# Causal attentions of a one-core transformer: the mask under the row maxima added by VectorE in the scores' bank instead of by TensorE's mask products

## The reference

```python
B_, S, D = (2, 256, 256); H = 16; HD = D // H
q = (x @ Wq.T).reshape(b, s, H, HD)
k = (x @ Wk.T).reshape(b, s, H, HD)
v = (x @ Wv.T).reshape(b, s, H, HD)
scores = jnp.einsum('bqhd,bkhd->bhqk', q, k) / np.sqrt(HD).astype(np.float32)
causal = jnp.tril(jnp.ones((s, s), bool))
scores = jnp.where(causal, scores, jnp.finfo(scores.dtype).min)
probs = jax.nn.softmax(scores, axis=-1)
out = jnp.einsum('bhqk,bkhd->bqhd', probs, v).reshape(b, s, d)
return out @ Wo.T
```

## Time and profile before

| what | value |
|---|---|
| runs of the kernel before | 2774.63, 2782.56, 2786.53 us, median 2782.56 |
| profiled execution | 2789.25 us, its span 2787.5 us |
| busy over the span: TensorE, VectorE, ScalarE, GpSimd | 2531.3, 1627.8, 1259.5, 1289.6 us |
| mean granted clock of TensorE | 0.928 of 2.4 GHz |
| layer 0's causal attention, first reduction to last maxima | about 57 to 226 us |
| layer 1's causal attention, the same | about 1458.5 to 1629 us |

### The profile page before, as it was taken

The page is one execution under the profiler, slowest core; times in us unless marked ns, Lnnn a source line. Parts: engine busy times, 40 slices in busy tenths (PEclk is TensorE's granted clock), DMA queues, the critical chain, the costliest instruction groups (busy, mean ns, idle before and its releaser), DMA issues. The chain is left out here.

```text
span 2787.5 us, 40697 instructions
## 1 busy us (share of the span) xinstructions
PE 2531.3 (91%) x14471; PEld 1686.6 (61%) x14474; DVE 1627.8 (58%) x2168; ACT 1259.5 (45%) x2174; POOL 1289.6 (46%) x1130
## 2 busy tenths in 40 slices
PE   6887999878999999999878888789999989998798
PEld 4444777654444444444664446578888867776676
DVE  4663555577666766664436633477767745554555
ACT  4464333464555555555334552256555543333222
POOL 4100344486888888888521003254545523442243
PEclk9798999898999999999976979899999998998799
DMA  1000111121101101010000001100100001110111
GB/s 58 1 2 15 35 46 48 44 79 38 39 16 38 39 24 38 16 35 1 27 24 1 1 1 49 52 22 20 31 20 20 21 10 41 45 45 15 30 42 41
DMA packets 39709, 81.63 MB, mean 29 GB/s; under 512 B 7552, under 2 KB 21120, under 8 KB 39040
## 3 DMA queue, kind: packets, MB, share of 16 engines
q1 hardware_dynamic: 39264, 79.41, 10.2%
q10 hardware_dynamic: 288, 0.13, 0.0%
HBM read 59.07 MB, written 2.62 MB: 22 GB/s over the span
## 5 line engine op out<-in xcount | busy, mean ns | idle before, releaser
L2017 DVE TENSOR_REDUCE a1h_mseg<-bank 128x2 f32<-128x1024 f32 x256 | 302.7, 1222 | 187.3 <-PE bank L1774 173.4
L63 POOL TENSOR_TENSOR f_wh<-f_raw,ones_r 128x768 fp32r<-128x768 f32 (+1 forms) x74 | 111.8, 1511 | 545.6 <-PE bank L464 367.2
L1951 ACT ACTIVATE a1h_prob<-bank 128x512 f32<-128x512 f32 x366 | 206.1, 598 | 165.8 <-PE bank L1834 83.8
L1754 POOL TENSOR_TENSOR a_qk<-a_qk,a1h_prob 128x512 f32<-128x512 f32 x186 | 238.7, 1315 | 50.8 <-ACT a1h_prob L1951 50.8
L453 PE MATMUL bank<-x_norm_h,f_wh 128*128 128x512 f32 x592 | 244.2, 412 | 6.5 <-PEq L3247 2.5
L453 PE MATMUL bank<-x_norm_l,f_wh 128*128 128x512 f32 x592 | 238.7, 403 | 0.0
L453 PE MATMUL bank<-x_norm_h,f_wl 128*128 128x512 f32 x592 | 237.5, 401 | 0.0
L656 DVE SCALAR_TENSOR_TENSOR f_tf<-bank,f_bias,f_sg 128x512 f32<-128x512 f32 x148 | 111.0, 751 | 191.8 <-PE bank L453 185.4
L1832 PE MATMUL bank<-a1h_ql,a1h_k 128*128 128x512 f32 x512 | 203.2, 397 | 0.0
L544 ACT ACTIVATE f_hhi<-f_hf 128x512 fp32r<-128x512 f32 x124 | 78.3, 632 | 276.3 <-DVE f_hf L664 276.3
L1847 PE MATMUL bank<-a1h_prob,a_v 128*64 128x512 f32 x732 | 179.8, 604 | 0.0
(11 more groups left out here) (595 smaller groups left out, 6337.8 us busy)
## 6 DMA issues: line engine op xcount, KB each, us to landing
f_raw<-in_l_w_dram SPq DMA_DIRECT2D x66, 385.0 KB, 3.1
a1h_st_q<-a_qk SPq DMA_DIRECT2D x128, 128.0 KB, 2.4
l2a_qkraw<-in_l2a_wqk_dram SPq DMA_DIRECT2D x32, 128.0 KB, 2.1
l2a_vraw<-in_l2a_wvg_dram SPq DMA_DIRECT2D x8, 512.0 KB, 3.8
f_raw<-in_l_w_dram SPq DMA_DIRECT2D x8, 449.0 KB, 3.3
a_qk<-l_keys SPq DMA_DIRECT2D x24, 128.0 KB, 2.8
a1p_raw<-in_l1a_w_dram SPq DMA_DIRECT2D x20, 128.0 KB, 2.1
a_qk<-in_l1a_wo_dram SPq DMA_DIRECT2D x16, 128.0 KB, 2.1
```

Of the source, the lines that this page charges most:

```text
L63: return pool.tensor_tensor(dst, src, one.to_broadcast(list(src.shape)), ALU.mult)
L1754: pool.tensor_tensor(out, first, slot_of[t % NP], ALU.add).then_inc(sum_done, 1)
L1951: act.activation(slot_of[t % NP], core.bank[2 + t % 3][:, :], ACT.Exp, scale=scale).then_inc(p_ready, 1)
L2017: dve.tensor_reduce(mseg[:, :, qb, s], spare(("A", n, k))[:, :, :], AX.X, ALU.max).then_inc(a_read, 1)
```

## The change

In a diagonal visit TensorE issues no mask products for the maxima any more. Each pair is announced by its score products. VectorE first adds a constant tile `later` (128 x 128, 0 on and under the diagonal, -1e30 above it, the same for both heads) to the last 128 columns of both heads, in their bank, waits for that addition, and then reduces as before. `later` is made by GpSimd with a memset and an affine select among the other constants.

```diff
@@ attend_causal
+        later_added, cleared = sem("later_added"), sem("cleared")
+        later = sb("later", [P, P])
@@ masks(pool, written)
             pool.memset(mpos[:, :, :, :].bitcast(F32), 0.0).then_inc(made, 1)
+            pool.memset(later[:, :], 0.0).then_inc(cleared, 1)
+            pool.wait_ge(cleared, 1)
+            pool.affine_select(later[:, :], later[:, :], [[-1, P]], ALU.is_ge, -1e30, base=0,
+                               channel_multiplier=1).then_inc(made, 1)
@@
+        def diagonals(x):
+            return sum(seg(y)[3] for y in range(x))
@@ maxima(x) on TensorE
-                                       kt[rows, 2 * (Q % SLOTS) + p, s * HALF:s * HALF + n], start=True, stop=not diag,
+                                       kt[rows, 2 * (Q % SLOTS) + p, s * HALF:s * HALF + n], start=True, stop=True,
                                        tile_position=(64 * u, 0))
-                    if not diag:
-                        mm.then_inc(a_ready, 1)
-                    elif x < 4:
-                        mask_pair(x, p, n)
-                if diag and x >= 4:
-                    for p in range(2):
-                        mask_pair(x, p, n)
-
-            def mask_pair(x, p, n):
-
-                ps = spare(("A", x, p))
-                for c in range(2):
-                    for u in range(2):
-                        mm = mask(pe, ps[:, u, n - P + 64 * c:n - P + 64 * c + 64], 0, c, u)
-                mm.then_inc(a_ready, 1)
+                    mm.then_inc(a_ready, 1)
@@ maxima(x) on VectorE
                     dve.wait_ge(a_ready, use["A", x, p] + 1)
+                    if diag:
+                        part = spare(("A", x, p))[:, :, n - P:n]
+                        dve.tensor_tensor(part, part, later[:, :].unsqueeze(1).to_broadcast([P, 2, P]),
+                                          ALU.add).then_inc(later_added, 1)
+                        dve.wait_ge(later_added, 2 * diagonals(x) + p + 1)
```

## The result

The changed kernel takes 2811.1 us, median of 6 runs (2802.9 to 2820.9), beside 2786.0 us of the kernel before on the same chip. The medians are 25.1 us apart, 0.90%. The changed kernel is slower, clear of noise. Forecast was 2789.5 us, no change that can be told, with a range up to 2807. The profiled execution took 2812.45 us, span 2810.7, granted clock 0.920 (before 2789.25, 2787.5, 0.928).

The account below looks back on a forecast made before the run. No engine was full; TensorE, VectorE and ScalarE hand work to each other. Per attention 2.1 + 3.1 - 2.0 = 3.2 us, 6.4 for both, plus 0.5 gave +6.9: 2782.56 to 2789.5 us, range 2775 to 2807.

Parts of the forecast that it names:

- Mid-unit visits: 0: Diagonal visits within units: reads about 0.3 us later, held by slack, cost 0; 6.3 us for 21 visits without that cover.
- VectorE becomes the pace: Rival: slack fails, every diagonal visit after the head costs 0.9 less at most 0.5; +27.1 us, 2810; chance 0.22.
- The unit starts, +0.45 each: Seven unit starts after the head: additions cost 0.90, 0.47 returns; 0.45 us each, +3.1 us an attention.
- The TensorE term: 256 mask products dropped per attention; waits for exponentials hide half of 28 visits, the rest gives -2.0 us.
- The price of an addition, 0.42 + 0.03: VectorE: each addition takes 0.42 us plus 0.03 for the wait behind it, 0.45 a pair, 28.8 us an attention.
- The head, +2.1: Visits 0 to 3 before unit 0's M: eight additions bring 3.6 us, idle time absorbs part, +2.1 us an attention.
- GpSimd, +0.5: Making the constant with memset and affine select delays layer 1's block by 0.5 us; nothing in layer 0.
- the fast rival: Rival: all masked idle time and mask products come back, 15 us less 0.5 gained, 2768; chance 0.08.
- this rival: Rival: TensorE's clock stays down longer, seven more half-clock steps in each attention, 8 us, 2797.5; chance 0.12.

Follow-up runs that it names:

- e7_mid: e2_pairwise with VectorE's additions in place of the masks only in diagonal visits neither in the head nor last of a unit (84 additions): 2787.4 us.
- e2_pairwise: The kernel before, all mask products kept, with each pair's masks right behind its score products in every diagonal visit, no additions: 2773.0 us.
- e6_last: e2_pairwise with VectorE's additions in place of the masks only in the last visit of units 1 to 7's maxima (28 additions): 2802.9 us.
- e1_no_add: The changed kernel without its 128 additions, so no mask under the maxima, and 1e-30 added to the sums: 2779.4 us.
- e3_dummy: The changed kernel with as many mask products as before, put ahead of the score products that overwrite them: 2811.6 us.
- e5_head: e2_pairwise with VectorE's additions in place of the masks only in visits 0 to 3 (16 additions): 2785.7 us.
- e8_fill: The changed kernel with unused filler products on TensorE ahead of each wait for the maxima: 2814.4 us.
- e11_tiny: The changed kernel with each addition over the last 4 of the 128 keys alone, and a small number added to the sums: 2792.8 us.

## Why the prediction was wrong

**The step that failed is "Mid-unit visits: 0".** It said that a step's slack, 1.24 us less 0.34, holds the lateness of VectorE's reads. That slack came from two late steps at full clock. e7_mid measured these additions alone at 11.8 us of attention (15.6 by the medians). I had worked out a loss of 6.3 if the cover were gone, and that for 21 visits: one attention's, so 12.6 for both. They lose in the first half of an attention: in layer 0 the stretches from one `add_maxima` to the next grow by 0.4, 2.4, 1.8 and 2.0 us against e2_pairwise up to unit 4's, and by nothing from there (-0.2, -0.4, -0.3). Steps 3 to 6, which hold two visits each, lie in the second of these stretches alone. What the three that grew most share is the clock: they run 10.6, 5.4 and 6.8 us longer at 1.2 GHz, the others no longer. In layer 1 the last two stretches run 9.7 and 3.4 us less at it, and there they are 2.4 and 1.1 us shorter than in e2_pairwise, with all their additions. Both attentions together have 119 us at 1.2 GHz instead of 85. At the price worked out below, 0.25 to 0.3 us for each, these 34 us are 9 to 10 of the 11.8. So the cover may well have held at full clock; what was put at nothing without a reason is that TensorE's extra waits in mid-unit (58.9 us of read-waits instead of 43.0) would come with more time at the lower clock. That the one causes the other no run isolates. The rival "VectorE becomes the pace", 2810 us with 0.22, named the right outcome, but not by its mechanism, every visit late by 0.4. That would be 16.8 us for the 42 visits of e7_mid, where 11.8 were measured, none of them in the second half of an attention, and 5.6 for the 14 unit starts of e6_last, where 21.8 were.

**The unit starts, +0.45 each, were mis-sized.** The tail of unit 7 did cost 0.44. But of these seven starts unit 7's is the only one where M follows the maxima directly, 0.4 us behind the start of the instruction that writes them to `mpos`. For units 1 to 6 it is 1.4 to 4.4 us behind, since it stands behind later users of the ring, in the start shown above behind the next visit's first pair. So no start but the last looks like the rows that I took the earlier trace rows. e6_last measured 21.8 us for 14 of them, 1.6 each (0.2 to 2.9 in the single stretches). I had taken 0.9 us of addition less 0.47 us returned; the two additions cost 0.9 to 2.2, and up to 0.9 comes on top where M runs at the lower clock. What is returned by the early announcement stands in e2_pairwise and is not theirs.

**What came back came from elsewhere.** The terms of the sum give back 0.47 for seven starts and 2.0 for TensorE's masks, 5.3 us an attention, 10.6 in all. e1_no_add measured 5.0 by the medians, 3.9 to 11.1 by the interval of its ratio, and 12.1 in the attentions of its profiled execution, so the size is not refuted. The TensorE term, -2.0 each, was found at nothing: e3_dummy, with all products, cannot be told from the changed kernel. (The reading behind it was wrong too: by the row the eight products end at 206.83, not at 206.66, which is also where 0.31 us of waiting before 207.13 puts them.) The other part is real: e2_pairwise brings 11.4 us by the announcement alone.

**The sum again.** I had charged additions with 16.8 us (2.1 and 7 x 0.9 for each attention) and 0.5 for GpSimd, less 10.6. Measured: 30.1 less 5.0.

**What held.** The price of an addition, 0.42 + 0.03: 0.426 and 0.03. The Trainium skill, "VectorE: DVE Perf Modes", section "The DRAIN you can't avoid", would have a semaphore between chained operations cost nothing over none; the rows above show 0.03 us of gap with one and 0.09 us of overlap without, here too. The head, +2.1: +1.9 to `add_maxima`. e5_head, though, lost 7.9 us in both attentions for twice that: 3.7 in layer 0's head, of which 7.8 us ran at 1.2 GHz, 1.8 in layer 1's, of which none did, and 2.5 behind the heads. GpSimd, +0.5: +0.59. And what I held against the fast rival, that idle time which is filled comes back as other idle time, is what the additions' row shows, 27.7 us.

**The clock** fell with the rest: 0.78 and 0.80 in the attentions (0.86 and 0.81 before, over the same stretches). Below 0.80 I had said that this rival is at work; it had 8 us, for seven more steps in each attention. One stretch shows it, from unit 3's `add_maxima` to unit 4's. The changed kernel, the stretch and its first half:

```profile
146.36:168.15 21.79, 18.29 (x96) 9.16 (x98) 11.60 (x22) 13.24 (x22) 0.00 (x0) 0.77 0.00 1
...
148.50:150.50 2.00, 1.69 (x6) 0.95 (x5) 1.91 (x4) 1.55 (x4) 0.00 (x0) 0.50 0.01 4
150.50:152.50 2.00, 2.00 (x14) 0.87 (x14) 0.25 (x1) 1.07 (x2) 0.00 (x0) 0.50 0.00 0
152.50:154.50 2.00, 1.80 (x8) 0.91 (x8) 0.98 (x2) 1.90 (x4) 0.00 (x0) 0.50 0.00 0
```

and e2_pairwise over the same unit:

```profile
139.65:157.30 17.65, 15.18 (x128) 8.11 (x131) 8.13 (x14) 13.25 (x22) 0.00 (x0) 1.00 0.00 1
```

The changed kernel spends about 10 us of this at 1.2 GHz, e2_pairwise none; before had 18.0 us at 1.00. In the 2 us ahead of the fall TensorE was busy for 1.42, and 1.25 in those in which it fell. But this fall is not the additions' doing alone. e1_no_add, which has none, runs as much of the same stretch at 1.2 GHz and takes 20.70 us, so that the additions add 1.1:

```profile
141.22:161.92 20.70, 18.28 (x96) 9.23 (x99) 8.13 (x14) 13.24 (x22) 0.00 (x0) 0.75 0.00 1
```

What the lower clock costs can be read from stretches of one execution, since both attentions run the same code (at full clock this stretch takes 18.04 us in either, before). First the last stretch of the kernel before, unit 6's `add_maxima` to unit 7's, in layer 0 and layer 1; then layer 1's counterpart of the changed kernel's 21.79 us:

```profile
199.23:223.03 23.80, 20.32 (x204) 9.73 (x203) 16.56 (x22) 15.15 (x32) 0.00 (x0) 1.00 0.00 1
1601.51:1627.86 26.35, 23.17 (x204) 11.70 (x203) 16.58 (x21) 15.27 (x32) 0.00 (x0) 0.84 0.00 1
...
1568.41:1588.32 19.91, 15.77 (x96) 8.13 (x99) 11.59 (x21) 13.24 (x22) 0.00 (x0) 0.91 0.00 0
```

8.4 us more at 1.2 GHz go with 2.55 us more, and 6.8 with 1.88: 0.3 us for each. Over the 35 pairs of such stretches in the 13 traces that differ by over 3 us in it, the fit is 0.25. From before to after the attentions' time at 1.2 GHz rises from 111 to 150 us, and these 39 us are then about 10 to 12 of the 21.0. A whole step of the earlier trace rows, 3.34 instead of 2.77 us, would give less, 39 x 0.57 / 3.34 = 6.7. Both are estimates: e8_fill did not isolate the clock, and the share of waits and clock is not settled beyond them.

## What to carry to other kernels

Slack is a property of one step of one unit. Before charging an addition at nothing, ask what TensorE's waits do to its clock, read the steps of the stretches that already run at the lower one, and list every user of the buffers that the slower reader frees, not the one nearest to the change. When a change bundles an earlier announcement with a moved piece of work, try the announcement alone: here it was the whole gain (2773.0 us), and the moved work the whole loss. Idle time in front of an engine is no budget when it and its producer wait for each other over two slots; 28.8 us of new work left 21.3 of 32.0 us of idle time standing. And where a part whose code is unchanged moves, compare its granted clock first: here that accounted for most of it.

## What the runs showed that I had not expected

A VectorE addition inside the bank over 128 x 8 elements still takes 0.169 us, over 128 x 128 0.293 and over 128 x 256 0.426: 0.16 us fixed and about 1.04 ns for an element of a row. So even the smallest keeps 0.17 us, and with e11_tiny's about half of the additions' loss stays (14.5 of 30.1 us). And M, the same eight products, took from 1.08 to 1.97 us by the clock granted there (outside e8_fill, where filler products run right ahead of it), and the length of TensorE's wait just ahead does not decide it: behind 1.98 us of waiting unit 7's M took 1.58 in the changed kernel and 1.08 in e6_last.
